# Turning the row maxima of an attention batch: one 128x128 transpose and one DMA in place of four 128x32 transposes and two DMAs

## The reference, cut to what matters

```
# x: 4 batches x 512 queries x 128 channels; ctx: 4 x 154 keys x 128; 16 heads of 8 channels
x = x + tanh(g_xattn[0]) * xattn0(layernorm(x), ctx)     # layer 0: plain attention
x = x + tanh(g_ffn[0])   * ffn0(layernorm(x))            # quantised gated feed-forward
x = x + tanh(g_xattn[1]) * xattn1(layernorm(x), ctx)     # layer 1: attention with a causal mask
x = x + tanh(g_ffn[1])   * ffn1(layernorm(x))            # a scan over the 4 batches

def xattn(q, ctx):
    s = (q Wq^T + bq) . (ctx Wk^T + bk) / sqrt(8)        # per head: 512 x 154
    return softmax(s) (ctx Wv^T + bv) Wo^T + bo          # softmax subtracts the row maximum
```

## Time and profile before

| what | value |
|---|---|
| median of 3 runs | 343.93 us (343.29 to 344.03) |
| profiled execution, first to last instruction | 341.2 us |
| around it, median less span | 2.7 us |
| instructions | 4468 |
| mean granted TensorE clock | 0.957 |
| TensorE busy | 279.0 us (82%) |
| VectorE busy | 252.5 us (74%) |
| ScalarE busy | 192.6 us (56%) |
| GpSimd busy | 136.7 us (40%) |

### The profile page before, as it was taken

How to read it: one execution, slowest core, us unless ns; L and a number is a source line. 1 busy time by engine, 2 the same in 40 slices (tenths; PEclk the granted TensorE clock), 3 DMA queues, 4 the chain that set the end, 5 groups by cost and what they waited for, 6 DMA issues and landing times. The chain is left out here.

```text
span 341.2 us, 4468 instructions
## 1 busy us (share of the span) xinstructions
PE 279.0 (82%) x1424; PEld 160.7 (47%) x1424; DVE 252.5 (74%) x538; ACT 192.6 (56%) x303; POOL 136.7 (40%) x274
## 2 busy tenths in 40 slices
PE   0889899899989779985007888899998998999994
PEld 0558544455434345331005776664654654444462
DVE  5699875877996388889989977986596693441834
ACT  1673367556476746779589632446656446665232
POOL 6669893750050411870002059921386207131100
PEclk9999999999999999997556999999999999999998
DMA  7930100010000000000000002220001000000004
GB/s 204 336 146 3 69 32 10 27 73 10 1 8 3 0 0 2 1 0 0 1 0 0 2 0 92 94 100 2 10 25 76 8 0 10 1 0 3 0 1 123
DMA packets 9687, 12.55 MB, mean 37 GB/s; under 512 B 896, under 2 KB 5376, under 8 KB 9664
## 3 DMA queue, kind: packets, MB, share of 16 engines
q1 hardware_dynamic: 9232, 11.80, 9.7%
q10 hardware_dynamic: 432, 0.47, 0.7%
HBM read 4.27 MB, written 1.05 MB: 16 GB/s over the span
## 5 line engine op out<-in xcount | busy, mean ns | idle before, releaser
L1333 DVE TENSOR_REDUCE sb_nm<-ps_top 128x3 f32<-128x462 f32 (+2 forms) x168 | 96.0, 626 | 26.6 <-PE ps_top L953 13.9
L772 ACT ACTIVATE sb_pr<-ps_score 128x512 f32<-128x512 f32 (+1 forms) x148 | 82.3, 583 | 58.8 <-PE ps_score L985 49.2
L953 PE MATMUL ps_top<-sb_Kd,sb_Q 128*128 128x462 f32 (+3 forms) x240 | 69.7, 349 | 4.7 <-DVE sb_nm L1333 2.4
L985 PE MATMUL ps_score<-sb_Q,sb_Kd 128*128 128x512 f32 x119 | 54.4, 467 | 1.3 <-ACT sb_pr L772 1.0
L953 PEld LDWEIGHTS ps_top<-sb_Kd,sb_Q 128*128 128x128 f32 x240 | 42.6, 188 | 18.1 <-DVE sb_nm L1333 11.9
L626 POOL TENSOR_SCALAR sb_var<-sb_mv 128x4 f32<-128x4 f32 x16 | 4.7, 291 | 83.3 <-DVE sb_mv L1296 82.9
L985 PEld LDWEIGHTS ps_score<-sb_Q,sb_Kd 128*128 128x128 f32 x119 | 22.2, 188 | 31.6 <-ACT sb_pr L772 23.4
L1017 PE MATMUL ps_pv<-sb_pr,sb_V 128*32 128x512 f32 x256 | 34.1, 605 | 0.0
L620 POOL TENSOR_SCALAR_AFFINE_SELECT sb_pr<-sb_pr 128x512 f32<-128x512 f32 x16 | 10.6, 661 | 46.4 <-ACT sb_pr L772 46.4
L1353 DVE STREAM_TRANSPOSE sb_oq<-ps_pv 128x512 f32<-128x512 f32 x16 | 10.8, 700 | 12.4 <-PE ps_pv L1017 12.3
L643 POOL TENSOR_SCALAR sb_xn<-sb_xr,sb_nmean,sb_rstd 128x128 f32<-128x128 f32 x44 | 19.3, 453 | 1.2
(11 more groups left out here) (180 smaller groups left out, 556.5 us busy)
## 6 DMA issues: line engine op xcount, KB each, us to landing
sb_Q<-sb_qh SPq DMA_DIRECT2D x16, 256.0 KB, 2.3
sb_Q<-sb_ql SPq DMA_DIRECT2D x8, 256.0 KB, 3.3
sb_xr<-x SPq DMA_DIRECT2D x4, 256.0 KB, 7.7
out<-sb_xr SPq DMA_DIRECT2D x4, 256.0 KB, 2.5
sb_wsb<-w SPq DMA_DIRECT2D x1, 704.0 KB, 9.0
sb_wf<-wffn SPq DMA_DIRECT2D x1, 576.0 KB, 8.6
sb_wkr<-wkr SPq DMA_DIRECT2D x2, 256.0 KB, 7.1
sb_Q<-sb_nmT SPq DMA_DIRECT2D x16, 32.0 KB
```

Of the source, the lines that this page charges most:

```text
L772: act.activation(pr[:, k % PRING, q0:T], score_bank(B * layer + b, t)[:, q0:T], ACT.Exp, scale=SCALE).then_inc(exp_r, 1)
L953: ins = pe.matmul(cols[:, c0:c1, :], Q4[n % 3][:, g, P * qt:P * qt + P], Kd[n % 3][:, g, j:j + c1 - c0, 0:keys], start=True, stop=not mask ...
L985: ins = pe.matmul(ps[:, :], Kd[n % 3][:, g, j, 0:P], Q4[n % 3][:, g, :], start=True, stop=True, skip_group_check=True)
L1333: dve.tensor_reduce(nm[:, :, :].rearrange("p t h -> p (t h)")[:, f0:f0 + heads], top[k % MRING][:, 0:keys * heads].rearrange("p (h k) -> p ...
```

## The change

The layout of `nms` becomes `[head in group, part, group, query tile]`, which is 128 numbers to a partition, and one transpose turns them all: row `32 j + 16 a + 4 g + t` of `nmT` then holds 128 queries of query tile `t`. The rows of the maxima in `Q4` are now 3, 19, 35, ... 115 (every 16th) and no longer 3 and 7 of each 32. With that one DMA reaches them all, for the maxima and for the zeros of `nil`. The counts of `m_in` and `q_in` follow, and a filler keeps the later tiles at their addresses. The order of instructions on each engine is as before, but for the three transposes and the DMAs that are gone.

```diff
-        nms = sb("nms", [P, TT, 2, J, G], F32R)
+        nms = sb("nms", [P, J, 2, G, TT], F32R)
...
-            nmT = sb_here("nmT", [32, 2, T], F32R)
+            nmT = sb_here("nmT", [P, 2, P], F32R)
+            sb_here("gap2", [P, 2 * T - 2 * P])
...
         def q_landed(n):
-            return q_in[n % 3], 16 * sum(5 if m in CLEAN_MAX_ROWS else 3 for m in range(n % 3, n + 1, 3))
+            return q_in[n % 3], 16 * sum(4 if m in CLEAN_MAX_ROWS else 3 for m in range(n % 3, n + 1, 3))
...
                 if n in CLEAN_MAX_ROWS:
                     sp.wait_ge(nil_r, 1)
-                    for a in range(2):
-                        sp.dma_start(Q4[n % 3][3 + PARTS * a:P:32, :, :].bitcast(F32),
-                                     nil[16 * a:16 * a + 16, :]).then_inc(q_in[n % 3], 16)
+                    sp.dma_start(Q4[n % 3][3:P:16, :, :].bitcast(F32), nil[:, :]).then_inc(q_in[n % 3], 16)
 
             def tops(layer, b):
                 n = B * layer + b
                 sp.wait_ge(nmT_r, n + 1)
-                for a in range(2):
-                    sp.dma_start(Q4[n % 3][3 + PARTS * a:P:32, :, :].bitcast(F32),
-                                 nmT[16 * a:16 * a + 16, n % 2, :].bitcast(F32)).then_inc(m_in[n % 3], 16)
+                sp.dma_start(Q4[n % 3][3:P:16, :, :].bitcast(F32).rearrange("p g (t q) -> p (g t) q", q=P),
+                             nmT[:, n % 2, :].bitcast(F32)).then_inc(m_in[n % 3], 16)
...
                 if n >= 2:
-                    act.wait_ge(m_in[(n - 2) % 3], 2 * 16 * ((n - 2) // 3 + 1))
-                act.activation(nmT[:, n % 2, :], misc[0:32, :], ACT.Copy).then_inc(nmT_r, 1)
+                    act.wait_ge(m_in[(n - 2) % 3], 16 * ((n - 2) // 3 + 1))
+                act.activation(nmT[:, n % 2, :], misc[:, 0:P], ACT.Copy).then_inc(nmT_r, 1)
...
-                for t in range(TT):
-                    ins = pe.transpose(misc[0:32, P * t:P * t + P],
-                                       nms[:, t, :, :, :].rearrange("p a j g -> p (a j g)").bitcast(F32), ident[:, :])
-                ins.then_inc(misc_full, 1)
+                pe.transpose(misc[:, 0:P], nms[:, :, :, :, :].rearrange("p j a g t -> p (j a g t)").bitcast(F32),
+                             ident[:, :]).then_inc(misc_full, 1)
...
                 if t == 0:
-                    pe.wait_ge(m_in[n % 3], 2 * 16 * (n // 3 + 1))
+                    pe.wait_ge(m_in[n % 3], 16 * (n // 3 + 1))
...
-                src = nm[:, :, :].rearrange("p t (g j) -> p t j g", g=G)
+                src = nm[:, :, :].rearrange("p t (g j) -> p j g t", g=G)
                 part = [nms[:, :, a, :, :] for a in range(2)]
```

## The result

The changed kernel took 339.22 us (median of 4, 338.85 to 339.97), the kernel before 343.73 us beside it (343.29 to 344.03): a ratio of 0.9877, 95% interval 0.986 to 0.9894, which is 4.2 us. Two more comparisons on two other chips gave 0.9911 (0.9889 to 0.9932) and 0.9866 (0.9848 to 0.9884). Over all 14 executions the changed kernel's mean is 339.6 us, that of 66 executions of the kernel before 343.3 us: 3.8 us. The forecast was 341.1 us, with a range of 340.1 to 342.9. The direction was right, and the forecast gain of 2.8 us was too small.

The account below looks back on a forecast made before the run. No engine is full; a relay of waits between VectorE, TensorE and ScalarE bounds it. Batch gains sum to 3.1 us, 2.8 after absorption: span 338.4 plus 2.7 around it, 341.1 us, range 340.1 to 342.9.

Parts of the forecast that it names:

- rival 1: Most of the gain absorbed behind GpSimd's normalising at batches 2, 3, 6, 7: 342.7 us; chance 0.19, 0.09 for no change.
- Rivals 2 (a late DMA): The single 64 KB DMA of the maxima lands late, some 1.5 us at each of eight batches: 353 us; chance 0.03.
- 3 (a slower split): VectorE's split slowed by its step of 16 numbers, 0.4 us per batch losing all; within no change's 0.09, plus 0.01 slower.
- Rival 4: DMA's wait at batch 0 and shorter waits at the ring of scores count too: up to 3.8 us, 340.1; no separate chance.
- Sum 3.1 us: Total of the gains forecast batch by batch over all eight batches.
- I let a tenth be absorbed: 2.8 us: Of the 3.1 us summed over the batches, a tenth is lost in the relay of engines, leaving 2.8 us.
- which comes 0.23 us earlier each: Batches 0 and 4: VectorE's first unit behind the transposes comes 0.23 us earlier each, 0.5 us together.
- the wait is not the bound and I give it nothing: Batch 0: TensorE's 0.27 us wait for the DMA counts nothing, since VectorE's reductions pace the units ahead.
- 0.46 us each: Exponential behind the copy starts 0.46 us earlier: 1.4 us over batches 5 to 7, 0.9 us over 2 and 3.
- an exponential holds it up: Batch 1: ScalarE's copy has no idle time ahead, so earlier transposes give nothing there.
- the copy's 0.33 us alone: Batch 1: only the shorter hold of ScalarE by the copy counts, 0.3 us.
- with the 2.7 us around it, which are taken from the median: Time outside the profiled span, 2.7 us, added to the forecast span of 338.4 us to give 341.1 us.

Follow-up runs that it names:

- E2: Changed kernel with ScalarE's copy 512 columns wide again, as before the change: 342.01 us, ratio 0.9955.
- E3: Changed kernel with the same 128x128 transpose done four times, three into columns nobody reads: 341.64 us, ratio 0.9954.
- E6: Changed kernel with four transposes, the 512 wide copy and two DMAs all back; only the new layout stays: 343.49 us, ratio 1.0006.
- E4: Changed kernel with the maxima sent by two DMAs of 32 KB in place of one of 64 KB: 339.39 us, ratio 0.9887.
- E5: The kernel before the change run again, no edit: 343.37 us, ratio 1.0003.
- E1: The changed kernel run again, no edit: 340.45 us, ratio 0.9911.
- E10: The changed kernel run a third time, no edit: 338.8 us, ratio 0.9866.
- E9: Changed kernel with transpose and copy one slot later (15), and in layer 0 the normalised batch's turning at slot 17: 339.16 us, ratio 0.9874.
- E8: Changed kernel with nine filler matmuls in place of five ahead of batch 0's transpose: 340.09 us, ratio 0.9915.
- E12: Changed kernel with transpose and copy one slot later (15) at batches 1, 5, 6 and 7 alone: 338.83 us, ratio 0.9862.

## Why the prediction was right and where it was wrong

**The mechanism was right.** The top is a relay from VectorE over TensorE to ScalarE; shorter transposes and a narrower copy shorten it, at every batch. E2 takes back 1.7 us, E3 2.1 us, E6 all. The absorption of rival 1 didn't happen: 0.02 to 0.06 of each 0.5 us. Rivals 2 (a late DMA) and 3 (a slower split) are refuted by the rows above. Rival 4, "more than said", is what came: it named the DMA's wait at batch 0 and up to 3.8 us.

**Step that failed: "Sum 3.1 us", "I let a tenth be absorbed: 2.8 us".** The terms were too small. They measure some 4.0 us; 0.3 are absorbed, as forecast, and 3.6 to 3.7 are left. Another 0.2 us outside the span, which the prediction put at nothing, makes 3.8 to 3.9. Term by term:

- Batches 0 and 4, *"which comes 0.23 us earlier each"*, and *"the wait is not the bound and I give it nothing"*. VectorE's wait ahead of its first reduction fell by 0.28 us at both (0.92 to 0.64, 1.18 to 0.90). At batch 4 that is all. At batch 0 it was 0.5 to 0.6: the 0.27 us of waiting for the DMA did count, and is gone. With transposes and copy short even two DMAs are in time (E4, split to first 4.83); with one DMA and four transposes there is no wait either (E3); with all three back it returns (E6).
- *"0.46 us each"* at batches 2, 3 and 5 to 7: measured 0.53 to 0.56. The one transpose lets the score follow 0.08 us behind it, not 0.14.
- *"an exponential holds it up"*, *"the copy's 0.33 us alone"* at batch 1: 0.42 us against the profile that was read, 0.46 against E5. The exponential of `t = 14` started at 51.19. In E1 the copy of batch 1 starts 0.49 us behind that exponential (51.10 to 51.59), so ScalarE was free for it at some 51.68. The copy started at 51.76, 0.64 us behind the first transpose, as at batch 6. It was the transposes that held it, by 0.08 us, and E3 gives back just 0.08 there. The rows of the kernel before:

```profile
51.12 0.61 PE L967 MATMUL ps_misc<-sb_consts,sb_nms 128*32 128x128 f32 x4
51.19 0.60 ACT L772 ACTIVATE sb_pr<-ps_score 128x512 f32<-128x512 f32 x1 [0.82 <-PE ps_score L985]
```

**"... with the 2.7 us around it, which are taken from the median".** This mixes two executions: E5 and the runs beside it put 1.97 us around the span of the kernel before, and 1.75 lie around the changed one's. For the forecast it cancels: 338.4 + 2.7 is 343.93 less 2.8. What it hid is that 343.93 us, the median of three, was a high base. The 66 executions of the kernel before have a mean of 343.3. So of the 1.9 us by which 341.1 was missed, 1.0 is the gain (3.8 us by the means in place of 2.8), 0.6 the base, and 0.3 that the four executions of the result lie below the changed kernel's mean of 339.6.

**What the range left out.** Its lower end, 340.1, is the gain of 3.8 us that did come, taken from the high base; that the result lies 0.9 us below it is in part chance. Single executions of the changed kernel differ by 2.5 us (338.7 to 341.4), by their start and their clock. What makes the whole spread isn't settled: the start explains 0.8 us between E1's and E10's profiles and the clock in batch 0 some 0.8 us in others, and no profile was taken of the 341.4 us execution.

## What to carry to other kernels

A small copy or transpose that stands between steps of a relay costs what it delays its successors, not its duration: price it by the distance between starts, and add the waits that follow. Where the gain is under 1%, set marks in the trace (here the first and the last exponential) and compare distances between them: they agreed to 0.02 us, where the clock had not fallen between them, while times scattered by 2 us. And never take what lies around a span from the median of other executions.

## What the runs showed of the hardware

- A single transpose of 128x128 lets the next matmul start 0.08 us behind it, though four of them hold the next weight load back by 0.39 us; and a 128x128 copy out of PSUM lets ScalarE's next instruction start 0.16 us behind its start where it takes 0.27.
- One DMA of 64 KB from `nmT` has its last packet 1.8 us behind its issue; of two of 32 KB (E4) the last packet ends 1.7 us behind the second issue and 2.3 behind the first.
- In the programs with one DMA for the maxima, the first statistics of the input started at 4.13 to 4.23 us (9 profiles); with two DMAs at 4.33 to 4.50 (5 profiles), though the input's DMA is issued at 0.79 us in all. The rows are those of the changed kernel and of the kernel before:

```profile
4.17 0.87 DVE L1289 BATCH_NORM_STATS2 sb_stat<-sb_xr 128x6 f32<-128x128 f32 x4 [0.98 <-DMA sb_xr<-x]
```

```profile
4.39 0.88 DVE L1293 BATCH_NORM_STATS2 sb_stat<-sb_xr 128x6 f32<-128x128 f32 x4 [1.20 <-DMA sb_xr<-x]
```

  Why is open. The time outside the span (1.97 against 1.75 us) doesn't go with it: E4 and E6 with two DMAs have 1.7 to 1.8.
- The stretch at half clock in batch 0 came in three of the twelve profiles of the change and its variants, and in neither of the two of the kernel before. TensorE had idled 0.8 to 0.9 us ahead of the transpose in the changed kernel with the fall (0.87) and without it (E10, 0.82) and in the kernel before (0.88), so that idling alone doesn't decide it. Another such stretch, 18.4 to 22.1 us, stands in the profiles of E1, E3 and E9 alone; their splits start at 34.95 to 35.06, those of E8 and E12 without it at 35.9, so what sets the start of batch 0 is open too.
